# The order of GpSimd's indirect stores and the second norm's root in an attention loop

## The reference

```python
h = _L0_tok_ref(x, ...)
h = h + _L0_attn_ref(_layernorm(h, axis=-1), ...)
h = h + _L0_ffn_ref(_layernorm(h, axis=-1), ...)

# attention
rhs = jnp.cumsum(kf[..., None, :] * vl[..., :, None], axis=0)
a = jnp.einsum('lbhdf,lbhf->lbhd', rhs, qf)
denom = jnp.einsum('lbhf,lbhf->lbh', qf, jnp.cumsum(kf, axis=0))[..., None]
a = a / (denom + EPS)

# experts
logits = x @ gate_w + gate_b
probs = jax.nn.softmax(logits, axis=-1)
topv, topi = jax.lax.top_k(probs, K)
comb = jnp.sum(topv[..., None] * jax.nn.one_hot(topi, E, dtype=x.dtype), axis=2)
h = jax.nn.gelu(jnp.einsum('bnd,edf->bnef', x, w1) + b1)
y = jnp.einsum('bnef,efd->bned', h, w2) + b2
ffn_out = jnp.einsum('bne,bned->bnd', comb, y)
```

## Time and profile before

| | us |
|---|---|
| time, median of 3 runs | 828.26 |
| time, lowest and highest | 824.99, 832.96 |
| span of the profiled execution, first to last instruction | 899.5 |
| busy in it: TensorE | 715.8 |
| VectorE | 500.2 |
| ScalarE | 438.2 |
| GpSimd | 434.6 |
| TensorE's granted clock, mean of the span | 0.854 |

### The profile page before, as it was taken

The page is one execution under the profiler, slowest core; times in us unless marked ns, Lnnn a source line. Parts: engine busy times, 40 slices in busy tenths (PEclk is TensorE's granted clock), DMA queues, the critical chain, the costliest instruction groups (busy, mean ns, idle before and its releaser), DMA issues. The chain is left out here.

```text
span 899.5 us, 17136 instructions
## 1 busy us (share of the span) xinstructions
PE 715.8 (80%) x4943; PEld 663.1 (74%) x4944; DVE 500.2 (56%) x1474; ACT 438.2 (49%) x852; POOL 434.6 (48%) x456
## 2 busy tenths in 40 slices
PE   2437679988888888888898139999997899999960
PEld 1306468987777778788787139999997899999950
DVE  1145336765555555555653137888889665656520
ACT  1134246654454444555540027777775666565630
POOL 7770023443333344344432435777776666565543
PEclk9657859998888888888885559999998999999985
DMA  8940501211111111111100022333332243443337
GB/s 204 192 104 19 177 23 41 59 44 43 33 38 34 36 38 42 34 42 42 34 22 22 21 44 47 61 62 62 58 60 44 46 73 73 78 73 84 57 45 140
DMA packets 63713, 55.08 MB, mean 61 GB/s; under 512 B 24345, under 2 KB 55520, under 8 KB 63664
## 3 DMA queue, kind: packets, MB, share of 16 engines
q0 software_dynamic: 19840, 23.53, 15.6%
q1 hardware_dynamic: 39344, 27.76, 12.1%
q10 hardware_dynamic: 4480, 3.21, 1.1%
HBM read 32.52 MB, written 25.10 MB: 64 GB/s over the span
## 5 line engine op out<-in xcount | busy, mean ns | idle before, releaser
L1149 POOL DMA_INDIRECT result<-e_y,e_tag x78 | 138.5, 1776 | 93.8 <-DVE e_y L1479 81.9
L1208 PE MATMUL e_yp<-x_w2s,e_hh 128*128 x468 | 140.9, 368 | 2.0 <-DVE e_y L1479 2.0
L612 PE MATMUL a_ab<-a_values,a_masked 128*128 (+1 forms) x768 | 114.4, 298 | 29.3 <-DVE a_masked L873 29.3
L612 PEld LDWEIGHTS a_ab<-a_values,a_masked 128*128 128x128 f32 x768 | 108.3, 216 | 38.2 <-issue 37.5
L1472 DVE TENSOR_TENSOR e_hl<-e_hid,e_hh 128x512 fp32r<-128x512 f32 x117 | 80.3, 691 | 87.3 <-ACT e_hh L1274 85.5
L1266 ACT ACTIVATE e_hid<-e_hidden,e_b 128x256 f32<-128x256 f32 x234 | 101.3, 476 | 51.7 <-PE e_hidden L1195 37.0
L1209 PE MATMUL e_yp<-x_w2s,e_hl 128*128 x468 | 118.2, 252 | 0.0
L1274 ACT CAST e_hh<-e_hid 128x512 fp32r<-128x512 f32 x117 | 72.4, 621 | 62.0 <-PE e_yp L1209 58.8
L1137 POOL DMA_INDIRECT e_x<-x_dram,e_tag x78 | 82.5, 1058 | 39.0 <-issue 22.2
L1208 PEld LDWEIGHTS e_yp<-x_w2s,e_hh 128*128 128x128 f32 x468 | 88.8, 190 | 2.3 <-issue 2.2
L1209 PEld LDWEIGHTS e_yp<-x_w2s,e_hl 128*128 128x128 f32 x468 | 90.3, 193 | 0.0
(11 more groups left out here) (250 smaller groups left out, 1649.6 us busy)
## 6 DMA issues: line engine op xcount, KB each, us to landing
a_raw<-in_ew SPq DMA_DIRECT2D x16, 288.0 KB
x_w2s<-in_ew SPq DMA_DIRECT2D x8, 384.0 KB
x_w2s<-in_ew SPq DMA_DIRECT2D x16, 192.0 KB
h_dram<-x_w2s SPq DMA_DIRECT2D x8, 384.0 KB, 2.7
a_hb<-h_dram SPq DMA_DIRECT2D x16, 192.0 KB, 2.4
result<-a_hb SPq DMA_DIRECT2D x16, 192.0 KB, 2.0
x_dram<-a_att SPq DMA_DIRECT2D x16, 192.0 KB
spec_dram<-e_space ACTq DMA_DIRECT2D x16, 192.0 KB
```

What stands on the lines that cost most here:

```text
L612: last = pe.matmul(beside(o + r * VW), masked[n % 2][:, r], own_and_zeros.unsqueeze(1).broadcast_to([P, 2, 2, VW]), start=n == 0 and r == ...
L1149: pool.indirect_dma_start(out=out, in_=y[:, j], in_offset=None, out_offset=bass.IndirectOffsetOnAxis(ap=tag[:, i % 8, j, 0:1].bitcast(U32) ...
L1208: pe.matmul(Y[:, j, 0:2 * D], hh[:, f, c], w(f, 2 * D), start=f == 0, stop=False, skip_group_check=True)
```

## The change

The block under `if choice` in GpSimd's `emit` moves from its end to its beginning, word for word; the other engines' programs stay as they are.

```diff
             def emit(i, one, two, tail, choice):
+                if choice:
+                    if not fixed(i) or i >= 4:
+                        pool.wait_ge(s["scattered"], 64 * (i - 3))
+                    wait_apart(pool, s["rows_ready"], 3 * (i - 2))
+                    for j in range(TJ):
+                        for k in range(2):
+                            pool.indirect_dma_start(
+                                out=tbl_dram, in_=entry[:, k, j], in_offset=None,
+                                out_offset=bass.IndirectOffsetOnAxis(ap=slot[:, k, j:j + 1], axis=0)
+                            ).then_inc(s["scattered"], 16)
                 if tail:
                     rstd("rstd2_ready", i - 2, mv2, rstd2, "tail", 5 * (i - 2) + 4)
                 if one:
...
                         rstd("rstd1_ready", i + 1, mv, rstd1, "norm_step", 5 * (i + 1) + 4)
                     low_part(i, 1)
-                if choice:
-                    if not fixed(i) or i >= 4:
-                        pool.wait_ge(s["scattered"], 64 * (i - 3))
-                    wait_apart(pool, s["rows_ready"], 3 * (i - 2))
-                    for j in range(TJ):
-                        for k in range(2):
-                            pool.indirect_dma_start(
-                                out=tbl_dram, in_=entry[:, k, j], in_offset=None,
-                                out_offset=bass.IndirectOffsetOnAxis(ap=slot[:, k, j:j + 1], axis=0)
-                            ).then_inc(s["scattered"], 16)
             sched(pool, emit)
```

## The result

The changed kernel took 902.62 us, median of 4 runs (896.0 to 909.37). Before took 826.62 us in the same comparison (824.16 to 832.96, 4 runs). The ratio is 1.0946, with a 95% interval of 1.0886 to 1.1006. The forecast was 848 us and slower: the direction held, and the time is 54.6 us above it and 38.6 above the upper end of the range (864).

The account below looks back on a forecast made before the run. TensorE alone was taken to bound the loop at about 17.9 us an iteration; a later root adds 13 x 1.3 = 16.9 us plus 3.3 in the drain, 20.2 on 828.26, so 848 us; range 838 to 856, eight in ten 820 to 864.

Parts of the forecast that it names:

- The sum: Attention loop 13 x 1.3 = 16.9 us plus drain 3.3 us: 20.2 us on 828.26, giving 848 us.
- What bounds the kernel now: Attention loop: TensorE alone bounds a timed iteration of about 17.9 us; 72.8 us of late reports come from recording.
- The stores and the root: GpSimd: four stores end 5.52 us behind VectorE's placing; the second norm's root follows, ending 2.8 us later.
- Who waits for it: VectorE's norm moves 1.9 us later, TensorE's turn of normed rows 1.15 us; 1.3 us taken per iteration.
- What goes: Stores leaving the bottom of GpSimd's iteration: VectorE's wait for their landing priced at 0, at most 0.5 us an iteration.
- the clock falls: Rival, chance 0.06: TensorE's new 1.3 us gap brings the lower clock, 13 x 3.3 + 20 = 63 us, 891 us.
- the late reports are real: Rival, chance 0.16: timed runs have TensorE's late reports too; 72.8 us go, 20 come: 776, or about 800 us.

Follow-up runs that it names:

- filling the gap: From the changed kernel: 16 extra unread identity turns on TensorE before its wait for the normed rows, from iteration 3 on; 840.94 us, ratio 1.0205.
- the low part waiting: From the changed kernel: GpSimd's first low part waits until VectorE has applied the second norm; 864.57 us, ratio 1.0454.

## Why the prediction was wrong, point by point

*The step that failed* is the price of the new gap on TensorE. The sum took it as waiting alone, 13 x 1.3 us, with "a clock near 1.00", and so put the clock's fall at nothing; the reason given was that the gap is a third shorter than the one of 1.98 us. Measured, the clock fell to 0.50 behind eight of thirteen gaps of 1.5 to 1.9 us, and that is 59.3 of the 74.1 us that the thirteen steps lost. A second term was missing: the norm's slowing beside GpSimd's low part, which made the gap 1.88 us instead of 1.19.

*What bounds the kernel now.* The reading of one iteration was right for a quiet trace: 17.9 us forecast, 18.14 measured. The conclusion "that the late reports belong to recording a profile" was false, but did not shift the sum. The reports are absent from one further trace of before and there in the other, both recorded, and where they are there the timed runs take 908 us. So the mismatch of 899.5 and 828 came most likely from another chip or state of it, a case that I had not named; on timed runs of 828 us the false reason still led to the right base.

*The stores and the root.* Stores 5.52 us behind the placing were forecast and 5.64 measured, the root right behind them. Right.

*Who waits for it.* A gap of 1.15 us in front of the turn and 1.3 us an iteration were forecast. Without contention 1.19 and 1.39 were measured. In the changed kernel it is 1.88 and 20.19 - 18.14 = 2.05. The term that was left out is the low part: once the root comes late, GpSimd's L527 no longer has a gap ahead of it and runs beside the norm that the root released, and the norm is slowed by 0.71 us. I had followed the move on each engine for itself.

*What goes.* The landing of the stores was priced at 0 to 0.5 us an iteration. Moving two of them shows a price of another kind: the 19.8 us of landing wait fall to 2.1 and the loop's thirteen steps are 11.4 us shorter (246.80 - 235.39), of which 9.1 are one iteration whose clock fell behind such a wait; the other twelve give 0.2 us each.

*The sum.* 13 x 1.3 = 16.9 us was the forecast's loop. Measured, with the clock kept by filling the gap, 261.60 - 246.80 = 14.8, or 23.9 if before's one fallen iteration (27.27 - 18.14 = 9.1) is set aside. The drain and what follows cost 6.7 us where 3.3 were forecast.

*The rival "the clock falls"* had the mechanism and was given 0.06 and 891 us. Its chance failed by the argument "the gap is a third shorter": the gap was 1.88 us, not 1.3, and at 1.19 the clock falls still in about half of the iterations. Its price failed too: 3.3 us an iteration was taken from an iteration of 23.87 us at 0.86, which is about 6.7 us at the low level (23.87 x 0.14 / 0.5); measured, the low level lasts 17 us and costs 27.66 - 20.19 = 7.5 us. That the sum came near the mark (891 against 902.6) is luck: 59.3 us of clock, in eight fallen iterations of 7.5, where 13 x 3.3 = 43 stood.

*The rival "the late reports are real"* was half right: they are real on some chips and the move takes them away there, yet the kernel is slower even there, since the clock costs more than they did in the trace of that chip.

## What to carry to other kernels

A wait of one or two microseconds on a TensorE that is otherwise never idle is to be priced twice: as the wait, and as the rest of the iteration at half the clock. The second came here in eight of thirteen iterations and was about three times the first (59 us against some 20). When an instruction is moved, look at what runs beside the one that it delays, for the partner may start together with it. And where a long burst has slack behind it on one side and a deadline on the other, try to split it before moving it whole: two of four stores first beat the old order in both sessions where it ran, and the new one in the session that had both.

## What the runs showed that I had not expected

- The clock at one and the same gap: 1.87 us at 314.86 left it at 1.00, 1.88 us at 335.07 brought it to 0.50 for 17 us in which TensorE did not idle. A gap's length alone does not decide. At 1.5 to 1.9 us the clock fell behind eight of thirteen gaps in the changed kernel's first trace and eleven of thirteen in its second, at 1.2 to 1.3 us (the low part waiting) behind six of eleven, and behind none of three of 1.0 us (two stores first, third chip).
- The late reports depend on the chip or its state, not on the program alone or the profiler: 0 and 41.5 us of "remote" waits at L784 in two traces of one kernel. With one store at the end there were none on a chip where before took 894 us, and with two none where it took 908. Why some chips have them stays open.
- Two stores at the end instead of four let nearly all of the landing wait go (19.8 to 2.1 us), not half.
- On the chips that have late reports, the part ahead of the loop is longer as well (161 to 175 us from the span's start to the first placing, against 144 to 148). Nothing was tried on this, but the traces show where some of it goes. In the tokens' part GpSimd issues 42 indirect loads one after another until about 60 us, and beside them TensorE starts the 32 matmuls of L262 within 7 to 13 us in the quiet traces and within 18 to 31 us in those of the other two chips. The profile of the kernel before is of the second sort (the first row is the changed kernel's, the second before's; the last numbers are the first and the last start):

```profile
L262 PE MATMUL tk<-x_w2s,t_w x32: 631/631/686, 32.6 to 45.9; 48*64 48x256 f32 x32
L262 PE MATMUL tk<-x_w2s,t_w x32: 376/376/583, 32.5 to 57.2; 48*64 48x256 f32 x32
```

So the disturbance stands beside GpSimd's indirect transfers in both places, and the profile of before has it in both.
